# A mixture-of-experts loop taken by two pairs of half blocks at a time, with four places of turned rows

## The reference

```
for each expert e (w1, w2: 512 x 128, w3: 128 x 512):
    h = silu(xt @ w1 + b1) * (xt @ w2 + b2)
    y = y + ge[:, None] * (h @ w3 + b3)
z = silu(xt @ sw1 + sb1) * (xt @ sw2 + sb2) @ sw3 + sb3      # shared expert
x = x + tanh(g_ffn) * (y + z)
```

## Time and profile before

| what | us |
|---|---|
| median of 3 runs | 947.96 (946.75 to 948.66) |
| the profiled execution's own time | 949.98 |
| its span | 948.2 |
| TensorE busy in it | 937.4 |
| VectorE busy | 674.4 |
| ScalarE busy | 399.1 |
| GpSimd busy | 271.2 |

### The profile page before, as it was taken

How to read it: one execution, slowest core, us unless ns; L and a number is a source line. 1 busy time by engine, 2 the same in 40 slices (tenths; PEclk the granted TensorE clock), 3 DMA queues, 4 the chain that set the end, 5 groups by cost and what they waited for, 6 DMA issues and landing times.

```text
span 948.2 us, 14241 instructions
## 1 busy us (share of the span) xinstructions
PE 937.4 (99%) x5022; PEld 767.7 (81%) x5022; DVE 674.4 (71%) x1136; ACT 399.1 (42%) x991; POOL 271.2 (29%) x251
## 2 busy tenths in 40 slices
PE   9999999999999999999999999999999999999998
PEld 7888888888888788888888988989889887775553
DVE  6977669766666854644658787787878778786666
ACT  6336544333333332312655454555545525323332
POOL 1262333424243143002213232222222203024653
PEclk9999999999999999999999999999999999999999
DMA  7645454444545545457848556375563409663447
GB/s 261 202 167 166 136 173 159 169 164 167 167 166 186 189 169 190 154 196 273 310 163 294 189 184 227 118 252 173 196 228 108 168 1 368 240 233 101 141 145 272
DMA packets 65621, 179.30 MB, mean 189 GB/s; under 512 B 7215, under 2 KB 11567, under 8 KB 64144
## 3 DMA queue, kind: packets, MB, share of 16 engines
q1 hardware_dynamic: 59952, 166.86, 50.3%
q0 software_dynamic: 3840, 10.49, 3.4%
q10 hardware_dynamic: 1760, 1.05, 0.4%
HBM read 119.66 MB, written 60.82 MB: 190 GB/s over the span
## 4 chain that ended last, share of the span: by engine, by line
PE 95%; DVE 3%; issue 1%; DMA 1%; ACT 0%; SPq 0%; DVEq 0%; ACTq 0%
PE ps_job L837 7%; PE ps_job L839 7%; PE ps_job L838 7%; PE ps_attn L1053 6%; PE ps_score L1025 6%; PE ps_attn L1299 5%; PE ps_turn L1039 3%; PE ps_score L897 3%; PE ps_score L899 3%; PE ps_score L898 3%; PE ps_attn L897 3%; PE ps_attn L899 3%; PE ps_attn L898 3%; PE ps_job L899 2%; PE ps_job L897 2%; PE ps_job L1311 2%
## 5 line engine op out<-in xcount | busy, mean ns | idle before, releaser
L770 POOL TENSOR_TENSOR score_bias<-mask_bias,pos_bias 128x1024 f32<-128x1024 f32 x32 | 76.9, 2402 | 294.2 <-DVE probs L1890 186.3
L1365 ACT ACTIVATE probs<-probs,neg_max 128x128 f32<-128x128 f32 x256 | 99.4, 392 | 95.6 <-DVE neg_max L1893 95.6
L731 POOL TENSOR_TENSOR w_sum<-w_raw 128x256 f32<-128x256 f32 x30 | 22.8, 761 | 178.1 <-PE ps_attn L899 76.9
L1053 PE MATMUL ps_attn<-pT,v_s 128*128 128x128 f32 x512 | 62.7, 276 | 2.0 <-issue 1.7
L1025 PE MATMUL ps_score<-kq_s 128*128 128x128 f32 x512 | 62.4, 275 | 0.0
L1053 PEld LDWEIGHTS ps_attn<-pT,v_s 128*128 128x128 f32 x512 | 59.8, 192 | 2.7 <-issue 1.9
L1025 PEld LDWEIGHTS ps_score<-kq_s 128*128 128x128 f32 x512 | 59.8, 192 | 0.2
L1917 DVE TENSOR_TENSOR acc<-ps_job,acc 128x512 f32<-128x512 f32 x56 | 37.9, 686 | 29.8 <-PE ps_job L839 29.7
L1890 DVE TENSOR_TENSOR probs<-ps_score,score_bias 128x512 f32<-128x512 f32 x64 | 43.7, 682 | 14.6 <-PE ps_score L1025 12.0
L1355 ACT ACTIVATE w_hi<-w_sum 128x1024 fp32r<-128x1024 f32 x30 | 31.8, 1061 | 52.6 <-POOL w_sum L736 52.6
L1355 ACT ACTIVATE pT<-ps_turn 128x512 f32<-128x512 f32 x64 | 34.5, 592 | 45.8 <-PE ps_turn L1039 45.8
(11 more groups left out here) (484 smaller groups left out, 2685.2 us busy)
## 6 DMA issues: line engine op xcount, KB each, us to landing
kq<-st SPq DMA_DIRECT2D x32, 1024.0 KB, 4.9
kq_s<-kq SPq DMA_DIRECT2D x64, 512.0 KB, 4.5
v_s<-v_all SPq DMA_DIRECT2D x8, 2048.0 KB, 10.7
w_raw<-wa_dram SPq DMA_DIRECT2D x31, 512.0 KB, 5.7
v_all<-st SPq DMA_DIRECT2D x24, 512.0 KB, 3.7
wo_raw<-wo_dram SPq DMA_DIRECT2D x8, 1024.0 KB, 7.0
ew_s<-ew_dram SPq DMA_DIRECT2D x4, 2048.0 KB, 12.8
v_raw<-wv_dram SPq DMA_DIRECT2D x11, 512.0 KB, 6.4
```

The costliest lines, as they stand in the source:

```text
L770: nc.gpsimd.tensor_tensor(score_bias[:], mask_bias[:], pos_bias[:, i % 2].unsqueeze(1).broadcast_to([P, B, P]), ALU.add).then_inc(bias_rea ...
L1053: last = nc.tensor.matmul(ps_attn[half][:, cols(b)], v_s[g % 2][:, BH * half + b, cols(j)], pT[:, half, cols(b)], start=True, stop=True)
L1365: last = nc.scalar.activation(probs[i % 2][:, half, b], probs[i % 2][:, half, b], ACT.Exp, bias=neg_max[:, i % 2, half, b:b + 1], accum_ou ...
```

## The change

The loops of TensorE, ScalarE and VectorE take two blocks per round. With j = 0, 2, 4 and so on, TensorE's round is: `turn_x(j+2)`, `turn_x(j+3)`, `turn_h(j-2)`, `turn_h(j-1)`, `block_h(j)`, `block_h(j+1)`, `block_y(j-2)`, `block_y(j-1)`. The turned rows get four places, `xbT[b % 4]`. ScalarE and VectorE follow; VectorE reads the owners of the blocks ahead between adding the bias and the gate, and copies weights at the end of a round and at the head of the next. GpSimd's and SyncE's programs are the same as before. The diff, cut to its core:

```diff
             def block_y(b, e):
                 k = b % 2
                 pe.wait_ge(hbT_sbuf, b + 1)
-                if b == NB - 1:
+                if b >= NB - 2:
                     pe.wait_ge(w_copied, NB + 1)
...
             turn_x(0)
+            turn_x(1)
             owners = []
-            for b in range(NB + 2):
-                if b + 1 < NB:
-                    turn_x(b + 1)
-                if b >= 2:
-                    turn_h(b - 2)
-                if b < NB:
-                    owners.append(owner_of(b))
...
-                    block_h(b, owners[b])
...
-                if b >= NB:
-
-                    for _ in range(4 if b == NB else 2):
+            for j in range(0, NB + 2, 2):
+                for b in (j + 2, j + 3):
+                    if b < NB:
+                        turn_x(b)
+                for b in (j - 2, j - 1):
+                    if b >= 0:
+                        turn_h(b)
+                for b in (j, j + 1):
+                    if b < NB:
+                        owners.append(owner_of(b))
+                        pe.wait_ge(xbT_sbuf, b + 1)
+                        pe.wait_ge(w_copied, b + 1)
...
+                        block_h(b, owners[b])
+                if j == 2:
                     pe.wait_ge(ew3_in, 16 * 4)
+                if j == NB:
+
+                    for _ in range(2):
                         nc.tensor.matmul(ps_turn[0][:, 0:P], ones[:], ones[:], start=True, stop=True)
-                if b >= 2:
-                    block_y(b - 2, owners[b - 2])
+                for b in (j - 2, j - 1):
+                    if b >= 0:
+                        block_y(b, owners[b])
...
             take_xbT(0)
+            take_xbT(1)
+            for j in range(0, NB + 2, 2):
+                for b in (j + 2, j + 3):
+                    if b < NB:
+                        take_xbT(b)
...
+                for b in (j, j + 1):
+                    if b < NB:
+                        act.wait_ge(hb_biased, b + 1)
+                        nc.scalar.activation(silu_b[b % 2][:], h_b[b % 2][:, 0:P], ACT.Silu).then_inc(silu_b_done, 1)
+                if j == NB:
+                    take_hT(NB - 2)
+                    take_hT(NB - 1)
+                for b in (j - 2, j - 1):
+                    if b >= 0:
+                        take_y(b)
...
+            for j in range(0, NB + 2, 2):
+                if j >= 2:
...
+                    copy_w3(j - 2)
+                    copy_w3(j - 1)
+
+                    if j < NB:
+                        take_hT(j - 2)
+                        take_hT(j - 1)
+                for b in (j, j + 1):
+                    if b < NB:
+                        add_bias(b)
+                        if b + 2 < NB:
+                            owners += [owner_of(2 * b + 4), owner_of(2 * b + 5)]
+                        gate_b(b)
+                for b in (j + 2, j + 3):
+                    if b < NB:
+                        copy_w12(b)
```

More of the change, by code:

```diff
@@ L332, in build @@
         gate_diag = place("gate_diag", [P, len(SUMMED), TOP, P], F32, at_attn + (XB - XB_FIRST + YB - 2) * D * 4)
-        assert (XB - XB_FIRST + YB - 2) * D + len(SUMMED) * TOP * P <= 2 * SH * T
+        at = at_attn + (XB - XB_FIRST + YB - 2) * D * 4 + len(SUMMED) * TOP * P * 4
+        xbT += [place(f"xbT{n}", [P, D], F32, at + (n - 2) * D * 4) for n in range(2, 4)]
+        assert (XB - XB_FIRST + YB - 2 + 2) * D + len(SUMMED) * TOP * P <= 2 * SH * T
         bias_all = place("bias_all", [P, E, 2 * P], F32, at_v)
@@ L1298, in block_h @@
                     for half, w in enumerate((ew12_s[:, e, c], w12_b[k][:, c])):
-                        last = nc.tensor.matmul(ps_attn[k][half * HB:(half + 1) * HB, 0:2 * P], xbT[k][:, cols(2 * c + half, HB)],
+                        last = nc.tensor.matmul(ps_attn[k][half * HB:(half + 1) * HB, 0:2 * P], xbT[b % 4][:, cols(2 * c + half, HB)],
                                                 w, start=(c == 0), stop=(c == C - 1))
@@ L1618, in take_xbT @@
                 act.wait_ge(xbT_psum, b + 1)
-                copy(xbT[k][:], ps_turn[k][:]).then_inc(xbT_sbuf, 1)
+                copy(xbT[b % 4][:], ps_turn[k][:]).then_inc(xbT_sbuf, 1)
             def take_y(b):
@@ L1634, in _ @@
             take_xbT(0)
[L1635 to L1642, removed]
+            take_xbT(1)
[3 more added lines that the diff above has]
+                        take_xbT(b)
+                if j == 0:
                     act.wait_ge(owner_ready, 1)
@@ L2171, in _, with add_bias @@
                 add_shared(t)
+            owners += [owner_of(2), owner_of(3)]
+            copy_w12(1)
             dve.wait_ge(bias_in, 16)
-            for b in range(NB + 2):
+            def add_bias(b):
                 k = b % 2
[L2176 to L2180, removed]
-                        dve.wait_ge(ew3_in, 16 * 4)
[L2182 to L2193, removed]
-                                               ALU.add)
-                    last.then_inc(hb_biased, 1)
-                    dve.wait_ge(silu_b_done, b + 1)
-                    V.tensor_tensor(h_gate_b[k][:], silu_b[k][:], h_b[k][:, P:2 * P], ALU.mult).then_inc(hb_gated, 1)
@@ new lines, in add_bias, with gate_b @@
+                dve.wait_ge(hb_psum, b + 1)
+                for half in range(2):
+                    some = slice(half * HB, (half + 1) * HB)
+                    last = V.tensor_tensor(h_b[k][some, :], ps_attn[k][some, 0:2 * P], bias_all[some, owners[2 * b + half]],
+                                           ALU.add)
+                last.then_inc(hb_biased, 1)
+            def gate_b(b):
+                k = b % 2
+                dve.wait_ge(silu_b_done, b + 1)
+                V.tensor_tensor(h_gate_b[k][:], silu_b[k][:], h_b[k][:, P:2 * P], ALU.mult).then_inc(hb_gated, 1)
@@ new lines, in _ @@
+            for j in range(0, NB + 2, 2):
+                if j >= 2:
+                    if j == 2:
+                        dve.wait_ge(ew3_in, 16 * 4)
+                    else:
+                        dve.wait_ge(yb_psum, j - 2)
+                    copy_w3(j - 2)
[12 more added lines that the diff above has]
+                        copy_w12(b)
```

15 lines of the change are left out of this document (4 added, 11 removed).

## The result

The changed kernel takes 962.13 us (median of 4 runs, 959.99 to 964.32), the kernel before on the same chip 947.52 (946.75 to 948.66). The ratio is 1.0153, 95% interval 1.0128 to 1.0179: slower, by 14.6 us. The forecast was 952.5 with a range of 947 to 957: the right sign, and far too little.

The account below looks back on a forecast made before the run. TensorE was taken to bound the kernel (chain 95%, 3.44 us a block). Its loop: -3.0 without gather waits, +6.8 with them, +3.8; VectorE's closing path 0.7 more, +4.5 on 947.96: 952.5 us, range 947.0 to 957.0.

Parts of the forecast that it names:

- Seams: TensorE's switches between whole array and halves: 26 round trips become 13, 0.30 us each, -3.9 us.
- Rival E: The 0.30 us belongs to each block, not to the seam, so -3.9 falls away: 953.9 us; chance 0.05.
- The start and the tail: Extra TensorE waiting: +1.3 us at the start, with 1.6 in the second round, and +0.5 before block 22's product.
- The sum of -3.0 without the ring: TensorE's loop end without gather waits: -3.9 seams, -0.9 fewer products of ones, +1.3 start, +0.5 tail.
- the VectorE row that I had costed at nothing: VectorE's closed loop through gates and weight copies: 6.5 us against TensorE's 6.58 a round, so no cost.
- rival A: Gathers come in time on GpSimd, so TensorE never waits for them: 945.8 us, faster; chance 0.10.
- VectorE's reads: Two owner-number reads between bias and gate: about 1.5 us from bias to gate, each gate 0.2 to 0.3 later.
- Rival D: VectorE's row is the bound: gathers in time, but reads lengthen rounds to 6.9 us, 949.3 us in all; chance 0.03.
- The ring: Buffers refilled by GpSimd's gathers: TensorE waits 1.7 us every second round, before blocks 9, 13, 17, 21; +6.8 us; chance 0.70.
- U+14.85: TensorE's start after the pair's last gather lands, 14.85 us after U, the second block's turns; two rounds give 13.15.
- Rival B: TensorE's waits lower its granted clock: 955.5 us with two such stretches, 958.5 with four; chance 0.09.
- Trainium skill's rule about VectorE's copies: GpSimd cannot write DMA descriptors during VectorE's float32 SBUF copies: 2 us per chain, +8, 960.5 us; chance 0.03.

Follow-up runs that it names:

- the run without gathers: Changed kernel without GpSimd's gathers of blocks 8 to 23, which compute on the first eight blocks' rows: 947.95 us, ratio 0.9995 to the kernel before.
- its control: Kernel before the change, with the same sixteen gathers of blocks 8 to 23 left out: 947.8 us, ratio 0.9999.
- run with fills: Changed kernel with TensorE products of ones in idle time: six before gather waits of blocks 9, 13, 17, 21, five before block 1's turned h: 963.2 us.
- thin copies: Changed kernel with VectorE's weight copies cut from block 2 on (a quarter of the first weights, 64 of 512 columns of the second): 964.45 us, one run.
- pairs2: Changed kernel, GpSimd issuing scatter, gather, pause, scatter, gather; the second scatter waits for the products of the next round's first block: 953.61 us, ratio 1.0057.
- spaced: Changed kernel; GpSimd in round j waits for block j+1's products, then gathers j+8 and j+9, then scatters j-2 and j-1: 952.44 us, ratio 1.0054.

## Why the prediction was wrong

**Seams: right in size.** A round was to last 6.58; rounds that wait for nothing last 6.56 in the run without gathers, against 6.87 for two blocks before. Rival E is out.

**The start and the tail: right without the clock.** The second round's waits in the run without gathers are 1.0 for the gate and 0.5 for turned rows, and the tail's 0.5 is there. By the end of block 5's products the new order is 0.2 us behind its control though it has saved 0.9 at three seams and done 0.4 less (0.86 of second products less, 0.44 of turns more), so the start costs about 1.5 instead of 1.3. In the changed kernel the first low stretch of the clock follows right on it, 1.7 more, a term that the sum had at nothing.

**The sum of -3.0 without the ring: too good.** In the run without gathers block 23's products end 1.2 earlier than in its control (930.76 against 931.96), and VectorE's last sums, which close the kernel, begin 0.7 earlier. TensorE's loop as a whole ends 1.5 earlier (935.62 against 937.15) where the sum had 3.0:

```profile
933.47 8.78 DVE L2225 SCALAR_TENSOR_TENSOR acc<-y_back,gate_f,acc 128x512 f32<-128x512 f32 x12
```

```profile
934.18 8.78 DVE L2199 SCALAR_TENSOR_TENSOR acc<-y_back,gate_f,acc 128x512 f32<-128x512 f32 x12
```

(above the changed order, below its control). The missing 1.5 is the start, 0.2 over its price, and three waits for weight copies, 1.2 in all: the VectorE row that I had costed at nothing with less than 0.1 to spare. So rival A, 945.8, could not have come true either.

**VectorE's reads: right.** Bias to gate takes 1.41 to 1.70 us where I had 1.5, in 19 of the 22 blocks that have reads there, and 1.25 in the other three. **Rival D** is no bound by itself, but it left no room: each late signal goes into the next gate and weight copy at full size.

**The ring: right as a mechanism.** 1.56 of waiting before block 9 and 1.55 before 13 against 1.7; later it spreads over blocks 16, 17, 19, 21 and 23, 8.5 in all against 6.8. The low number of places in the old order costs 5.3 us by the same mechanism.

**The step that failed** is the one in which the four DMAs "run in a row". I priced that row only by when its last gather lands, U+14.85, and took TensorE's signals beside it to be on time. The longest wait, 2.09 before block 19's turns, shows what the row does besides, in a cycle with no low clock. Block 15's turns begin at 902.71, which is U. The next products end at U+4.42, where I had 4.43, but they end beside the third and fourth DMA of a row (906.18 and 907.50) and their update comes at 909.31, 2.18 late. VectorE, GpSimd and TensorE behind it:

```profile
909.45 0.86 DVE L2193 TENSOR_TENSOR h_b<-ps_attn,bias_all 64x256 f32<-64x256 f32 x2 [2.02 <-remote]
```

```profile
911.93 1.33 POOL L821 DMA_INDIRECT y_rows<-y_out,row_of  x1 [3.41 <-ACT y_out L1363]
...
916.23 1.02 POOL L804 DMA_INDIRECT xb<-x_rows,token_of  x1 [0.31 <-issue]
```

```profile
920.55 0.66 PE L1283 MATMUL ps_turn<-ident,xb 128*128 128x128 f32 x4 [2.09 <-DMA xb<-x_rows,token_of]
```

The bias starts 2.32 behind its products instead of 0.13, and all that hangs on it comes 2.2 later. The row takes 4.30 instead of 4.08 from its first scatter to its last gather, the landing with TensorE's start 4.32 instead of 3.75. So the cycle lasts 17.84 instead of 14.85, and 2.2 of the 3.0 are the late update. The late updates stood in none of the rivals. The kernel before shows no late one, and beside its loop GpSimd issues more than two DMAs in a row only once, three gathers from 854.05 to 857.71, beside which the updates of 856.44 and 857.03 were on time.

The second term that the sum had at nothing is the clock. The cycle from block 9's turns to block 13's was to be 14.85 too and took 17.2, and there no late update has a part: 1.7 is the low clock, 0.4 stands before the first product, where an owner's read shows behind the turned h, 0.4 between block 7's products and their bias, though the update came in time (883.46), and 0.2 in the row of DMAs; the landing was 0.4 shorter. Rival B had the low clock at 9 in 100, in the sense of two to four stretches; three came. The run with fills shows that they do not simply add to the ring.

In the loop of the changed kernel the waits for gathers (8.5), the clock (5.1) and the other waits of TensorE (5.6 against 1.2 before) come to 18; with -4.8 for seams and ones that leaves 13.2 of the 16.2 us explained. Another 0.8 is where VectorE's last sums begin: 2.2 ahead of TensorE's last sums (952.92) instead of 3.0, much as forecast (0.7). Where the other 2 are I have not settled.

How the 14.6 us divide, by runs: taking away the waits for gathers gives 4 to 5 back (with a longer row at the start); rows broken up as far as I could get it give about 5 more, the clock's share in it; the last 3.6 to 5.6 stayed with every such version that keeps the gathers. None beats the kernel before, and the six versions meant to win the loss back ended 3.4 to 8.1 us above what I had expected of them by theory R or G. How much of the 14.6 the late updates cost by themselves is therefore not shown; that GpSimd's gathers and their rows cost all of it is, by the two runs without gathers.

What stays open: why TensorE's updates are held. The runs show that it is frequent from the third DMA of a row on and rare before, that it is there with two gathers and two scatters a round, in the old order too, and not with the two scatters alone, that the kept updates come out in a burst, and that VectorE's copies are not needed for it. They do not show which resource the updates share with the DMAs, nor whether it takes gathers or only the length of the row: no run has scatters alone in rows of four through the loop. On the Trainium skill's rule about VectorE's copies, which I had weighed (page "SBUF — State Buffer", section "SBUF: two separate sides"), the thin copies agree with it in part: a DMA instruction beside four copies is 0.2 to 0.5 us longer, not by the 2 us of the copies.

## What to carry to other kernels

When a change groups an engine's work in pairs, it also groups everything that hangs on its results: look at what row of DMA instructions GpSimd will have to issue at once, and price not only the landing of the last but the signals of the other engines beside it. Here 0.3 us saved a round did not pay for the slack that the change took from a ring of buffers; count the rounds between the release and the use of a place in both orders first. An engine with less than 0.1 us a round to spare is a bound as soon as anything else is late, so give such a "costs nothing" a price in the range.

## What the hardware showed unexpectedly

- TensorE's semaphore updates can come long after the work: 4.3 us in a row of seven gathers, 0.2 to 2.3 in rows of four, 0.4 in two rows of two (`pairs2`), none over 0.2 in the kernel before. In the row of seven the held updates came out 0.06 us apart.
- In the profile this looks like an idle VectorE or ScalarE that waits for a TensorE instruction that has ended, or for "remote": a bias starts 0.71 (changed kernel, 873.73) or 1.96 us (`spaced`, 871.38) behind the end of its products instead of 0.15.
- The first scatter of a row takes 1.26 to 1.54 us in seven of nine rows beside VectorE's copies of weights, and 1.02 or 1.03 with the copies cut down.
- The clock fell to 1.2 GHz for 3.4 us behind single waits of TensorE of 1.1 to 1.6 us, and did not behind others of 1.1 and 2.1 in the same trace. With the first filled by products of ones it did not fall there, and the time stayed.
